# Graph network kernel on one core: the product P in three one-pass parts, transposes and Q one step earlier, other first loads

## The reference

```
H   = (adj != 0);  w = adj[0, :];  Dn = 1 / (H @ w);  Be = 1 / column sums of H
conv(x, W, b) = Dn * (H @ (Be * (H.T @ (x @ W.T)))) + b
h   = layer_norm(relu(conv(x, W1, b1))) * gamma + beta      # 512 wide
x1  = plain_norm(x + (conv(h, W2, b2) + x))                 # 256 wide
agg = (adj @ x1) / max(rowsum(adj), 1e-6)
out = plain_norm(x1 + relu([x1, agg] @ WL.T))
```

## Time and profile before

| | |
|---|---|
| Median of three runs | 1110.5 us (1110.23 to 1110.59) |
| Profiled execution: its time, its span | 1110.66 us, 1108.6 us |
| Busy: TensorE, VectorE, ScalarE, GpSimd | 1093.2, 699.6, 314.9, 182.5 us |

### The profile page before, as it was taken

The page is one execution under the profiler, slowest core; times in us unless marked ns, Lnnn a source line. Parts: engine busy times, 40 slices in busy tenths (PEclk is TensorE's granted clock), DMA queues, the critical chain, the costliest instruction groups (busy, mean ns, idle before and its releaser), DMA issues.

```text
span 1108.6 us, 18544 instructions
## 1 busy us (share of the span) xinstructions
PE 1093.2 (99%) x6112; PEld 899.0 (81%) x6112; DVE 699.6 (63%) x1846; ACT 314.9 (28%) x705; POOL 182.5 (16%) x256
## 2 busy tenths in 40 slices
PE   7999999999999999999999999999999999999997
PEld 6879697796978969688796887969789697887966
DVE  4665595665955768548685486754766646856326
ACT  4342302422124221333113331143301433024220
POOL 0222004120031202211031110401104020041000
PEclk9999999999999999999999999999999999999999
DMA  7017612067211572124611445115442075300001
GB/s 280 20 39 153 150 41 58 0 151 152 55 40 31 120 151 57 38 65 101 146 47 38 96 102 121 41 38 129 103 89 71 4 151 115 65 9 1 1 1 39
DMA packets 64599, 86.18 MB, mean 78 GB/s; under 512 B 9024, under 2 KB 54720, under 8 KB 64576
## 3 DMA queue, kind: packets, MB, share of 16 engines
q1 hardware_dynamic: 63520, 85.88, 33.6%
q10 hardware_dynamic: 1056, 0.00, 0.1%
HBM read 77.47 MB, written 8.39 MB: 77 GB/s over the span
## 4 chain that ended last, share of the span: by engine, by line
PE 94%; DVE 4%; DMA 1%; ACT 0%; issue 0%; ACTq 0%; DVEq 0%
PE bank L731 40%; PE bank L802 10%; PE bank L840 10%; PE bank L862 10%; PE bank L824 10%; PE bank L759 10%; PE bank L832 3%; PE bank L848 1%; DVE adjT L539 1%; DMA small<-in_L_gnn_gamma_dram 1%; DVE HT L544 1%; PE bank L768 1%; DVE o_f L676 0%; DVE xres L680 0%; ACT m_hi L389 0%
## 5 line engine op out<-in xcount | busy, mean ns | idle before, releaser
L731 PE MATMUL bank<-yv,adjT 128*128 128x257 f32 x1024 | 223.3, 380 | 0.0
L731 PEld LDWEIGHTS bank<-yv,adjT 128*128 128x128 f32 x1024 | 194.1, 190 | 31.3 <-issue 3.8
L394 ACT ACTIVATE small<-mv,small 128x1 f32<-128x1 f32 x192 | 56.6, 295 | 362.6 <-DVE mv L521 266.9
L759 PE MATMUL bank<-x_hi,H 128*128 128x258 f32 x512 | 122.8, 289 | 0.8 <-DVE m_lo L526 0.8
L731 PE MATMUL bank<-x_hi,H 128*128 128x256 f32 x512 | 122.6, 283 | 0.0
L731 PE MATMUL bank<-m_hi,HT 128*128 128x256 f32 x512 | 121.6, 281 | 0.0
L731 PE MATMUL bank<-x_lo,H 128*128 128x256 f32 x512 | 121.1, 281 | 0.0
L731 PE MATMUL bank<-m_lo,HT 128*128 128x256 f32 x512 | 120.9, 280 | 0.0
L526 DVE SCALAR_TENSOR_TENSOR m_lo<-bank,small,m_hi 128x256 fp32r<-128x256 f32 x128 | 61.1, 483 | 94.2 <-ACT m_hi L389 94.1
L824 PE MATMUL bank<-W1T,zT 128*128 128x512 f32 x256 | 120.4, 593 | 0.0
L840 PE MATMUL bank<-gW2T,xnT 128*128 128x256 f32 x512 | 119.8, 380 | 0.0
(11 more groups left out here) (80 smaller groups left out, 1621.7 us busy)
## 6 DMA issues: line engine op xcount, KB each, us to landing
raw<-in_adj_dram SPq DMA_DIRECT2D x112, 256.0 KB, 8.5
adjB<-in_adj_dram SPq DMA_DIRECT2D x224, 128.0 KB, 3.4
x_in<-in_x_dram SPq DMA_DIRECT2D x28, 256.0 KB, 4.5
out_dram<-xres SPq DMA_DIRECT2D x112, 64.0 KB, 1.6
raw<-in_adj_dram SPq DMA_DIRECT2D x4, 1024.0 KB, 12.9
w_row<-in_adj_dram SPq DMA_DIRECT2D x8, 512.0 KB, 3.7
x_in<-in_x_dram SPq DMA_DIRECT2D x1, 1024.0 KB, 7.1
out_dram<-xres SPq DMA_DIRECT2D x4, 256.0 KB, 2.2
```

The costliest lines, as they stand in the source:

```text
L394: nc.scalar.activation(std[:, i:i + 1], mv[:, which, i, 1:2], ACT.Sqrt, bias=eps_c)\
L731: last = mm(bank(stage, i)[:, 0:n_cols], lhsT, rhs, start=(k == 0 and part == 0), stop=(k == NT - 1 and part == parts - 1))
L759: last = mm(*args, start=(c == 0 and n == 0), stop=(c == NT - 1 and n == 1))
```

## The change

For P, z is rounded to z_high (ScalarE), z_low = z - z_high and z_cross = z_high - 4096 z_low (VectorE); W1 has three such parts, made once. One step has now two products: M(s) = z_cross @ W1_cross (two matmuls) into a bank of its own, and P(s) = z_high @ W1_high + z_low @ W1_low (four matmuls), all float32r. ScalarE scales M into `hbias`, GpSimd adds b1 to it, and VectorE's scale-and-add of P takes `hbias` in place of the bias row.

The normalization of h is no longer applied to `hrow`: W2 is centred once and Q is scaled by the inverse deviation on its way out. Nor is x1 centred before TX: WL is centred, and V's eviction scales; ScalarE normalizes `xres` afterwards. LAG_T goes from 3 to 2, LAG_Q from 4 to 3, and hrow's slots from 4 to 3. The second chunk of S2 lies in steps 0 and 1 (five and three of its eight k) instead of 0 to 3 (3, 2, 2, 1). The next graph's w row is loaded behind the first quarter of adj. In the set-up WL is loaded and centred first, W2 is centred by GpSimd and ScalarE and transposed late, and TensorE's transposes of adj run one tile later.

The diff, cut:

```diff
-    "P": (0, 1, 2, 0, 1, 2, 0, 1),
-    "Q": (3, 4, 5, 3, 4, 5, 3, 4),
+    "P": (0, 1, 0, 1, 0, 1, 0, 1),
+    "M": (2, 3, 2, 3, 2, 3, 2, 3),
+    "Q": (4, 5, 4, 5, 4, 5, 4, 5),
-SECOND_CHUNK = {0: (0, 1, 2), 1: (3, 4), 2: (5, 6), 3: (7,)}
-LAG_T = 3
-LAG_Q = 4
-H_SLOTS = 4
+SECOND_CHUNK = {0: (0, 1, 2, 3, 4), 1: (5, 6, 7)}
+LAG_T = 2
+LAG_Q = 3
+H_SLOTS = 3
...
 # SyncE, per graph
-                    sp.wait_ge(dn_ready, b * NT + NT)
-                    load_w(b + 1)
...
-                    load_graph(b + 1)
+                    load_raw(b + 1, 0)
+                    load_w(b + 1)
+                    for j in range(1, NT // 2):
+                        load_raw(b + 1, j)
 # GpSimd, per step s
+                    if s < NT:
+                        pool.wait_ge(*emptied("M", s, b))
+                        nc.gpsimd.tensor_tensor(hbias[:, s % 2, :], hbias[:, s % 2, :], b1_row[:, :], ALU.add)\
+                          .then_inc(hbias_done, 1)
+                    if s > LAG_Q:
+                        split_q(s - LAG_Q - 1)
 # ScalarE, set-up
-            for c in range(NT - 1):
+            for c in range(NT):
                 take_adjT(c)
...
+                if c == 5:
+                    sum_W2_beta()
+                if c == 6:
+                    centre_W2()
             take_m_hi("S1", 0, 0, 0)
 # ScalarE, per step s
+                    if s == max(SECOND_CHUNK):
+                        take_z_high(1)
                     if s < NT:
-                        act.wait_ge(*emptied("P", s, b))
-                        nc.scalar.activation(hrow[:, s % H_SLOTS, :], hrow[:, s % H_SLOTS, :], ACT.Relu)\
-                          .then_inc(relu_done, 1)
...
+                        act.wait_ge(*full("M", s, b))
+                        empties_bank(nc.scalar.activation(hbias[:, s % 2, :], bank("M", s)[:, :], ACT.Identity,
+                                                          scale=rDn_cross[:, s:s + 1]), "M", s)
+                    if s > LAG_Q:
+                        take_x_hi(s - LAG_Q - 1)
+                    if 0 <= s - 1 < NT:
+                        root("h", 0, std_h, s - 1, b)
 # (xnT copy unchanged, then the relu)
 # VectorE, per step s
+                    if s == max(SECOND_CHUNK):
+                        take_z_low(1)
+                    if s > LAG_Q:
+                        take_q(s - LAG_Q - 1)
+                    if 0 <= s - 1 < NT:
+                        dve.wait_ge(relu_done, b * NT + s)
+                        moments("h", 0, hrow[:, (s - 1) % H_SLOTS, :], s - 1, b)
...
                     if s < NT:
                         dve.wait_ge(*full("P", s, b))
+                        dve.wait_ge(hbias_done, b * NT + s + 1)
...
+                    if s == max(SECOND_CHUNK):
+                        take_z_cross(1)
```

More of the change, by code:

```diff
@@ L147, in graph_net @@
+        z_low, _, nxt = place("z_low", [P, ND, C], F32R, nxt)
+        z_cross, _, nxt = place("z_cross", [P, ND, C], F32R, nxt)
         hrow, _, nxt = place("hrow", [P, H_SLOTS, DH], F32, nxt)
-        xnT, _, _ = place("xnT", [P, 2, NH, P], F32, nxt)
+        assert nxt <= raw_at + 4 * NT * C
+        xnT, _, _ = place("xnT", [P, 2, NH, P], F32, w_row_at)
+        HB_TILE = NT // 2
+        hbias, _, _ = place("hbias", [P, 2, DH], F32, x_lo_at + 4 * HB_TILE * D)
         adjB, _, _ = place("adjB", [P, NT, NB, RB], F32, raw_at)
-        yv, _, _ = place("yv", [P, NT, YP], F32, HT_at)
@@ L462, in graph @@
                     act.wait_ge(*full("V", i, b))
-                    empties_bank(nc.scalar.activation(yv[:, i, 0:2 * D], bank("V", i)[:, :], ACT.Copy), "V", i)
+                    act.wait_ge(rstd_done["1"], b * NT + i + 1)
+                    empties_bank(nc.scalar.activation(yv[:, i, 0:2 * D], bank("V", i)[:, :], ACT.Identity,
+                                                      scale=rstd_1[:, i:i + 1]), "V", i)
                     if i + 2 < NT:
                         take_x1T(i + 2)
+                act.wait_ge(neg_mean_done, b + 1)
+                for i in range(NT):
+                    nc.scalar.activation(xres[:, i, :], xres[:, i, :], ACT.Identity, scale=rstd_1[:, i:i + 1],
+                                         bias=neg_mean_1[:, i:i + 1]).then_inc(normed["1"], 1)
                 for i in range(NT):
@@ L606, in graph, with take_z_low @@
                 dve.wait_ge(bias_loaded, 16 * 2)
-                dve.wait_ge(rDn_ready, b + 1)
-                for s in range(NT + LAG_Q):
+                dve.wait_ge(rDn_ready, b * 2 + 2)
+                def take_z_low(ch):
+                    for d in range(ND):
+                        dve.wait_ge(z_high_done, b * (NCH * ND) + ch * ND + d + 1)
+                        cols = slice(ch * CH, (ch + 1) * CH)
+                        empties_bank(nc.vector.tensor_tensor(
+                            z_low[:, d, cols], bank("S2", ch * ND + d)[:, :], z_high[:, d, cols].bitcast(F32),
+                            ALU.subtract), "S2", ch * ND + d)
@@ new lines, in take_z_cross, with take_q @@
+                def take_z_cross(ch):
+                    for d in range(ND):
+                        dve.wait_ge(*emptied("S2", ch * ND + d, b))
+                        cols = slice(ch * CH, (ch + 1) * CH)
+                        nc.vector.scalar_tensor_tensor(
+                            out=z_cross[:, d, cols], in0=z_low[:, d, cols].bitcast(F32), scalar=-SPLIT,
+                            in1=z_high[:, d, cols].bitcast(F32), op0=ALU.mult, op1=ALU.add).then_inc(z_cross_done, 1)
+                def take_q(i):
+                    dve.wait_ge(*full("Q", i, b))
+                    if i >= 2:
+                        dve.wait_ge(q_split, b * NT + i - 1)
+                    dve.wait_ge(rstd_done["h"], b * NT + i + 1)
+                    empties_bank(nc.vector.scalar_tensor_tensor(
+                        out=q_f32[:, i % 2, :], in0=bank("Q", i)[:, 0:D], scalar=rstd_h[:, i:i + 1],
+                        in1=bW2_row[:, :], op0=ALU.mult, op1=ALU.add), "Q", i)
@@ L617, in graph @@
[L617 to L626 removed]
+                            out=hrow[:, s % H_SLOTS, :], in0=bank("P", s)[:, :], scalar=rDn_main[:, s:s + 1],
@@ L648, in graph @@
                             dve.wait_ge(stats_done, b * NT + i + 1)
[L649 removed]
+                        inverse_root("1", std_1, rstd_1, i - 1, b)
                     if i < NT:
```

334 lines of the change are left out of this document (202 added, 132 removed), and 8 rows, old and new, of the table PRODUCT_BANKS.

## The result

The changed kernel takes **1127.9 us** (median of 4 runs, 1127.63 to 1128.78) against 1110.37 us for the kernel before, timed beside it (4 runs): ratio 1.0161, 95% interval 1.0143 to 1.0178. It is 1.6% slower, inside the range of the prediction (1103 to 1132) and 8 us above its 1120. The profiled executions' spans are 1126.0 us and 1108.6 us, 17.4 apart.

The account below looks back on a forecast made before the run. TensorE, busy 1093.2 of 1108.6 us, was taken as the bound, with its saving given back in waits. 1110.66 + 3 (stages) + 6.5 (set-up) = 1120.2, median 0.16 lower: 1120 us, range 1103 to 1132.

Parts of the forecast that it names:

- a longer addition of b1: Rival, chance 0.10: GpSimd's add in the loop lasts 1.6 us or more, R = 3.7, +2.7 a graph, 1139 us.
- TensorE's work: P/Q stage: six float32r matmuls take 1.40 us instead of 1.72, saving 0.32 a tile, 2.56 a graph, 20.5 in all.
- The loop, R = 3.37 us: P/Q stage: hbias, GpSimd's add, hrow and relu follow each other, 3.37 us a round; TensorE's own step is 3.57.
- Q(0) waits behind root(1): Start of Q: xnT(0) stands on ScalarE behind root(1), which waits for tile 1's moments; TensorE waits 1.7 us.
- Q(6): End of the P/Q stage: the late loop delays copy xnT(6), so TensorE waits near 1.1 us.
- The stage, 46.4 against 45.97: S2's start to S3's start: the saving goes in waits; 0.4 us more a graph, 3 us over eight.
- The bound below: Third stage: from Q(0)'s start at 23.15, TensorE alone needs 22.1 us and ends at 45.3, -0.7 a graph.
- the loop is short enough: Rival, chance 0.20: R is 3.2 and TensorE alone sets the stage; -0.7 to -1.1 a graph, 1104 to 1111 us.
- The set-up, +6.5 us (+3 to +9): First graph's S1: more ScalarE and GpSimd work delays the first m_lo, then W2's transposes and bias product; +6.5 us.
- z_high, z_low and z_cross lie behind S2's first half ... at nothing: Ahead of M(0): their 4 us for the first chunk are covered by 4.67 us of S2, costing nothing.
- The w row: Next graph's load, behind 1 MB of adj: later adj quarters come up to 3.7 us later, at no cost.
- Only z_cross has two: Steady step: other VectorE instructions have at most one SBUF input; given as argument against the much longer GpSimd add.

Follow-up runs that it names:

- e6: Changed kernel with ScalarE taking hbias(s+1) ahead of relu(s), xnT ahead of both and the root last; GpSimd's add kept: 1104.99 us, ratio 0.9956 to before.
- e8: e6 with the set-up of e7 and VectorE's four last sums of Dn moved earlier: 1097.98 us, ratio 0.9892 to the kernel before.
- e1: Changed kernel with GpSimd's addition of b1 to hbias left out: 1115.35 us, ratio 1.0047 to the kernel before.
- e2: Changed kernel with ScalarE's copy xnT(s-2) ahead of the root of h(s-1): 1120.19 us, ratio 1.0103 to the kernel before.
- e4: Changed kernel with GpSimd's eight set-up instructions moved to VectorE: 1129.95 us, ratio 1.0192 to the kernel before.
- e7: e4 with VectorE's products also giving the row sums, W2 centred behind m_hi(0) to m_hi(3) and transposed behind S1(7): 1122.85 us, ratio 1.0116 to before.
- e5: Changed kernel with the edits of e3 and e2, and GpSimd's first residual held until VectorE's first z_cross: 1107.6 us, ratio 0.9979 to before.
- e10: e6 with the root of h(s-1) put back ahead of xnT(s-2), as in the changed kernel: 1139.23 us, ratio 1.0263 to before.
- e3: Changed kernel with hbias, scale and bias together, made by one VectorE instruction instead of ScalarE's and GpSimd's: 1134.68 us, ratio 1.0233 to before.
- e9: e8 with VectorE's rBe(0), rBe(1), m_lo(0) ahead of W1_cross and two more sums, and ScalarE's m_hi(0), m_hi(1) ahead of the last adjT: 1097.09 us.

## Why the prediction was right, point by point

The steady stage was right in mechanism and size, but it is only 3.5 of the 17.4 us. The rest lies in the set-up and the first graph, where the forecast was too low. That the total still lies in the range is in part luck: its upper part was room for a longer addition of b1, which did not come.

- **TensorE's work, M and P 1.40 instead of 1.72.** Right: from Q to Q TensorE's step is 3.57 us (350.28 to 353.85), 1.40 beside the 0.44 and 1.73 of the earlier trace rows; and once nothing waits, e6 and e8 have a stage of 43.4, 2.4 us under the kernel before, where 2.56 was predicted. The 216 ns for 512 columns of the Trainium skill (TensorE: Matmul & The Clock Gate, Back-to-back issue gap) are not seen: the records stand 0.233 us apart.
- **The loop, R = 3.37 us.** Right: 3.38. The add was put at 1.25 and is 1.28; hbias is 0.67. One reading was off, with no effect: an addition of 256 columns was said to last at least 0.726 us, and the earlier trace rows has one of 0.64. That this loop makes the end of the stage late is shown by e1 and e6, which open it in two ways.
- **Q(0) waits behind root(1).** Right as a mechanism (e2 takes it away), its size 1.24 us where 1.7 was predicted. Q(6) waits 0.88, predicted 1.1.
- **The stage, 46.4 against 45.97.** Right: 46.38, by the same reading. The saving of 2.56 was there and was given back in waits.
- **The bound below, "TensorE alone, 45.3".** This held only with the 1.7 us at Q(0) kept. The rival "the loop is short enough" was priced with it; had the loop been short and `xnT` free, the price would have been e6's: 2.4 a graph.
- **The set-up, +6.5 us (+3 to +9).** This is the term that was mis-sized: the first S2 is 9.8 us later, above the upper bound. S1(6) starts at 42.70 instead of 35.86, +6.8, near the upper end of what was said for it (39.1 and 0 to 4 more). The 0 to 4 were 3.2: ScalarE's m_hi(0) starts at 41.66 where the sum gave 38.2, and ScalarE had waited 1.76 and 1.13 us for GpSimd's products and 0.34 for TensorE. e4, without the two engines holding each other up, starts it 2.4 earlier. W2's transposes and the bias product add 1.3, as counted, and nothing of all this was caught up. The clock behind the wait, 0.50 for 3.3 us, was not thought of: S1(6) alone lost 1.6 us by it. ScalarE's copies ahead of m_hi(0) were counted; with them behind it, and their sums made by VectorE, e7 gains 1.7 more, which is within the scatter of the first S2.
- **"z_high, z_low and z_cross lie behind S2's first half ... at nothing".** True in the third graph, false in the first, where M(0) waits 3.40 us. The cover of 4.67 us was counted, but not that in the first graph VectorE's last four sums of Dn and Dn's reciprocal stand ahead of z_low and that the residual on GpSimd, which now runs beside them, stretches them (from 1.21 to 1.23 us each to 1.44 to 1.57, and the pair of z_cross from 1.28 to 1.76). e5 shows that: held back, 0.60 is left. e7 shows the share of the queue: with the sums nearer to S2's start, 1.19 is left. This is the second of the missed terms. With the first, 9.8 + 4.1 = 13.9 us against 6.5 + 0.4; it makes nearly all of the distance from 1120 to 1128.

The w row, the normalization of `xres` and the residual of the later graphs cost nothing in the changed kernel, as said: no wait of TensorE falls to them. For the w row this held by little: in the profiled executions of e6, e7 and e8 its later load cost 1.7 to 2.2 us in the first graph. "Only z_cross has two" SBUF inputs in the steady step was named as the reason why GpSimd and VectorE would not meet; e10 shows what it costs when they do, 1.1 us of wait in each graph.

## What to carry to other kernels

A change that makes the bounding engine's share shorter is paid out only if the loop through the other engines is shorter still; add that loop up instruction by instruction, and look for the queue in which the next turn's first instruction stands behind this turn's last. Two moves in ScalarE's queue were worth 23 us here. Two orders that seem independent may not be: hbias ahead was a gain with `xnT` first and a loss without, because it moved a GpSimd instruction onto a VectorE one that the other order had made critical. And where a first-graph stage is "as in the steady state", list what stands in each queue ahead of it only that once.

## What the runs showed of the hardware

- A wait of TensorE can cost twice. Behind waits of 5.84, 4.59, 3.68, 2.99 and 2.32 us the granted clock was 0.50 for some 3 us (behind that of 2.99 from 1.4 us after its end on) and the matmuls took 1.6 us more or over. It is not the length alone: after 1.89 us (e3) the clock stayed up in the first four graphs and fell in the last four; after 3.40 us it stayed at 1.00 in the changed kernel, e2 and e10 and fell in e1, e3, e4 and e6. Nor is it the program: the wait of 1.94 to 1.97 us for H in the set-up, with the same instructions ahead of it, was followed by 1.00 in the changed kernel, e3 and e5 and by 0.50 in e1, e2, e6 and e10. What decides was not tried.
- VectorE's H and HT columns beside GpSimd's operations of 512 columns took 1.77 us instead of 0.69, its sums of Dn 2.29 instead of 1.21, a z_cross 1.77 instead of 0.68. The Trainium skill (SBUF — State Buffer, Who interferes with whom) says that such pairs block each other, and the trace agrees.
- In all six kernels in which VectorE had more code than in the changed one (e3, e4, e5, e7, e8, e9) queue 14 fetched 41 packets of instructions instead of 10 to 12, and in the second graph VectorE stood idle ahead of z_low for reasons that the profile doesn't name: 5.59 us in e4, 4.36 in e5, 4.54 in e8. Part of that idle time is there in later graphs too; in e4 z_low starts 12.3 us behind S2's start in the second graph and 9.4 in the third. TensorE waited 0.3 to 2.2 us for it, once. That the fetch is the cause was not tested.
